# One semaphore per group for a GRU step's events, and PSUM zeroing moved behind tanh

## What is computed

```python
def step(hprev, gxt):
    gh = hprev @ whh.T + bhh
    r = jax.nn.sigmoid(gxt[:, :h] + gh[:, :h])
    z = jax.nn.sigmoid(gxt[:, h:2 * h] + gh[:, h:2 * h])
    n = jnp.tanh(gxt[:, 2 * h:] + r * gh[:, 2 * h:])
    hn = (1.0 - z) * n + z * hprev
    return (hn, hn)
...
fwd = _bigru(x_inner, ...)
bwd = jnp.flip(_bigru(jnp.flip(x_inner, 1), ...), 1)
y = jax.nn.silu(fwd + bwd) * jax.nn.silu(z)
```

## Time and profile before

| | |
|---|---|
| median of three executions | 1217.28 us |
| the profiled execution | 1218.96 us |
| its span, first to last instruction | 1217.2 us |
| mean granted TensorE clock | 0.582 of full speed |
| busy: PE, PE weight loads, DVE, ACT, POOL | 1088.6, 860.1, 948.2, 773.7, 154.8 us |
| recurrence of L2, first to last h_hi scan | 293.5 to 721.9 us |
| recurrence of L3, first to last h_hi scan | 765.2 to 1193.2 us |

### The profile page before, as it was taken

The page is one execution under the profiler, slowest core; times in us unless marked ns, Lnnn a source line. Parts: engine busy times, 40 slices in busy tenths (PEclk is TensorE's granted clock), DMA queues, the critical chain, the costliest instruction groups (busy, mean ns, idle before and its releaser), DMA issues. The chain is left out here.

```text
span 1217.2 us, 57599 instructions
## 1 busy us (share of the span) xinstructions
PE 1088.6 (89%) x22424; PEld 860.1 (71%) x22424; DVE 948.2 (78%) x5703; ACT 773.7 (64%) x4503; POOL 154.8 (13%) x222
## 2 busy tenths in 40 slices
PE   3787799949999999999999989999999999999997
PEld 2554354445888888888887866788888888888876
DVE  3543699987888888888888876788888888888884
ACT  4224530007777777777777764777777777777773
POOL 1001379920000000010001000000000001000100
PEclk9587899957555555555555556555555555555555
DMA  4000500000000000000000000000000000000000
GB/s 120 2 1 12 131 1 1 1 2 6 4 4 3 4 4 4 4 3 4 4 3 4 4 3 6 4 4 4 3 4 4 4 3 4 4 4 4 4 4 27
DMA packets 8235, 12.72 MB, mean 10 GB/s; under 512 B 5745, under 2 KB 7121, under 8 KB 7674
## 3 DMA queue, kind: packets, MB, share of 16 engines
q1 hardware_dynamic: 7962, 9.05, 3.0%
HBM read 8.26 MB, written 0.79 MB: 7 GB/s over the span
## 5 line engine op out<-in xcount | busy, mean ns | idle before, releaser
L1074 DVE TENSOR_TENSOR_SCAN L2s_h_hi<-L2s_renew,L2s_terms 96x32 f16<-96x32 f32 x512 | 113.2, 221 | 71.1 <-ACT L2s_terms L1134 9.3
L1074 DVE TENSOR_TENSOR_SCAN L3s_h_hi<-L3s_renew,L3s_terms 96x32 f16<-96x32 f32 x512 | 113.2, 221 | 70.9 <-ACT L3s_terms L1134 9.3
L1182 PE MATMUL L3s_reset_sum<-L3s_h_hi,L_w_hidden 97*128 97x8 f16 x2048 | 141.0, 179 | 20.9 <-DVE L3s_h_hi L1074 8.9
L1182 PE MATMUL L2s_reset_sum<-L2s_h_hi,L_w_hidden 97*128 97x8 f16 x2048 | 141.0, 179 | 20.5 <-DVE L2s_h_hi L1074 8.4
L1182 PEld LDWEIGHTS L3s_reset_sum<-L3s_h_hi,L_w_hidden 97*128 97x128 f16 x2048 | 94.5, 107 | 78.7 <-DVE L3s_h_hi L1074 32.0
L1182 PEld LDWEIGHTS L2s_reset_sum<-L2s_h_hi,L_w_hidden 97*128 97x128 f16 x2048 | 94.5, 107 | 78.5 <-DVE L2s_h_hi L1074 31.2
L1109 POOL TENSOR_TENSOR L_y<-L_states 96x64 f32<-96x64 f32 x128 | 40.8, 353 | 857.1 <-DVE L_states L1076 857.1
L1125 ACT ACTIVATE L3s_reset<-L3s_reset_sum 96x16 f32<-96x16 f32 x512 | 92.4, 181 | 67.0 <-PE L3s_reset_sum L1182 7.6
L1125 ACT ACTIVATE L2s_reset<-L2s_reset_sum 96x16 f32<-96x16 f32 x512 | 92.4, 181 | 66.7 <-PE L2s_reset_sum L1182 6.8
L1134 ACT ACTIVATE L2s_terms<-L2s_cand 96x16 f32<-96x16 f32 x512 | 111.2, 217 | 30.9 <-DVE L2s_cand L1059 4.5
L1134 ACT ACTIVATE L3s_terms<-L3s_cand 96x16 f32<-96x16 f32 x512 | 111.3, 217 | 30.1 <-DVE L3s_cand L1059 3.4
(11 more groups left out here) (257 smaller groups left out, 3522.7 us busy)
## 6 DMA issues: line engine op xcount, KB each, us to landing
L_wih_raw<-in_L_wih SPq DMA_DIRECT2D x2, 1152.0 KB, 11.3
l_w_raw<-in_L_w SPq DMA_DIRECT2D x1, 1296.0 KB
L_w_hidden_raw<-in_L_whh SPq DMA_DIRECT2D x2, 576.0 KB
stream<-in_x SPq DMA_DIRECT2D x2, 384.0 KB, 3.9
out<-stream SPq DMA_DIRECT2D x4, 192.0 KB, 2.1
l_idft<-in_idft SPq DMA_DIRECT2D x1, 400.0 KB
rpe_lw<-in_rpe_lw SPq DMA_DIRECT2D x1, 384.0 KB
l_dft<-in_dft SPq DMA_DIRECT2D x1, 288.0 KB, 2.9
```

The source lines that it names most:

```text
L1074: e.tensor_tensor_scan(flat(h_hi[g][0:C, x]), flat(renew[g][:, x]), flat(terms[g][:, x]), 0.0, ALU.mult, ALU.add).then_inc(hi_ready[g], 1)
L1182: return e.matmul(dst, weights.hidden[0:rows, wp, GATES * (2 * g + j) + gate, :], rhs, start=False, stop=False, skip_group_check=True)
```

## The change

Four edits, all in gru_steps.

1. The semaphores activated and cand_summed, and the kept part's raise of updated, become one semaphore per group, advanced. It is raised five times a step: by TensorE when the candidate's sum is complete, by ACT behind the reset sigmoid, the keep sigmoid and tanh, and by DVE behind the kept part. The candidate waits for the second of them, the kept part for the third, new_state for the fifth, each with a single wait. The semaphore updated is raised once a step.
2. The two copies of zeros no longer stand between renew sigmoid and tanh of step 0. The copy for the reset bank stands behind tanh of step 0, that for the keep bank behind tanh of step 1.
3. TensorE waits for each copy on a new semaphore, zeroed. In step 1 of these chunks it takes the gates in the order CAND, KEEP, RESET and waits ahead of RESET; in step 2 it keeps the order RESET, CAND, KEEP and waits ahead of KEEP.
4. The input products ahead for KEEP are spread over steps 2 to 7 of a chunk instead of 1 to 7.

The candidate's result stays in SBUF, as before.

```diff
-        reset_summed, keep_summed, cand_summed = each("reset_summed"), each("keep_summed"), each("cand_summed")
-        activated, cand_ready = each("activated"), each("cand_ready")
+        reset_summed, keep_summed = each("reset_summed"), each("keep_summed")
+        advanced, cand_ready = each("advanced"), each("cand_ready")
         updated, hi_ready, lo_ready = each("updated"), each("hi_ready"), each("lo_ready")
+        zeroed = each("zeroed")
+        RESET_ZEROED, KEEP_ZEROED = 0, 1
...
-                    e.wait_ge(activated[g], 3 * q + 1)
-                    e.wait_ge(cand_summed[g], q + 1)
+                    e.wait_ge(advanced[g], 5 * q + 2)
...
-                    e.wait_ge(activated[g], 3 * q + 2)
+                    e.wait_ge(advanced[g], 5 * q + 3)
                     e.tensor_tensor(terms[g][:, x, :, 1], keep[g][:, x], states[g][:, q, :, 1], ALU.mult)\
-                        .then_inc(updated[g], 1)
+                        .then_inc(advanced[g], 1)
...
-                    e.wait_ge(activated[g], 3 * q + 3)
-                    e.wait_ge(updated[g], 2 * q + 1 + BEFORE[g])
+                    e.wait_ge(advanced[g], 5 * q + 5)
...
-                    e.wait_ge(updated[g], 2 * q + 2 + BEFORE[g])
+                    e.wait_ge(updated[g], q + 1 + BEFORE[g])
...
-                    renewed = s == 0 and 1 <= q // STEPS < CHUNK_COUNT - 1
+                    renewed = 1 <= q // STEPS < CHUNK_COUNT - 1
...
-                        if renewed:
-                            e.activation(reset_sum(g, 1 - p)[0:C], zeros[:], ACT.Copy)
-                            e.activation(keep_sum(g, 1 - p)[0:C], zeros[:], ACT.Copy)
-
                         e.wait_ge(cand_ready[g], q + 1)
-                        e.activation(terms[g][:, x, :, 0], cand[g][:, x, :, 1], ACT.Tanh).then_inc(activated[g], 1)
+                        e.activation(terms[g][:, x, :, 0], cand[g][:, x, :, 1], ACT.Tanh).then_inc(advanced[g], 1)
+                        if renewed and s == RESET_ZEROED:
+                            e.activation(reset_sum(g, 1 - p)[0:C], zeros[:], ACT.Copy).then_inc(zeroed[g], 1)
+                        if renewed and s == KEEP_ZEROED:
+                            e.activation(keep_sum(g, 1 - p)[0:C], zeros[:], ACT.Copy).then_inc(zeroed[g], 1)
...
-                        for gate in (RESET, CAND, KEEP):
+                        before, at = divmod(q - 1, STEPS)
+                        zeroing = 1 <= before < CHUNK_COUNT - 1 and at in (RESET_ZEROED, KEEP_ZEROED)
+                        for gate in (CAND, KEEP, RESET) if zeroing and at == RESET_ZEROED else (RESET, CAND, KEEP):
+                            if zeroing and gate == (RESET if at == RESET_ZEROED else KEEP):
+                                e.wait_ge(zeroed[g], 2 * (before - 1) + (1 if at == RESET_ZEROED else 2))
                             for j in range(2):
                                 add(gate, 0, 0, j)
                                 add(gate, 1, 0, j)
-                        ahead(RESET, 1)
+                        ahead(RESET, RESET_ZEROED + 1)
...
-                        add(CAND, 0, 1, 1).then_inc(cand_summed[g], 1)
-                        ahead(KEEP, 1)
+                        add(CAND, 0, 1, 1).then_inc(advanced[g], 1)
+                        ahead(KEEP, KEEP_ZEROED + 1)
```

More of the change, by code:

```diff
@@ L1046, in _ @@
                 e.wait_ge(prepared, PREPARED)
-                for s, n in ((updated[1], 2), (hi_ready[0], 1), (hi_ready[1], 1), (lo_ready[0], 1)):
+                for s, n in ((updated[1], 1), (hi_ready[0], 1), (hi_ready[1], 1), (lo_ready[0], 1)):
                     e.sem_inc(s, n)
-                BEFORE = (0, 2)
+                BEFORE = (0, 1)
                 def candidate(g, q):
@@ L1093, in _ @@
                     new_state(1, q)
-                e.wait_ge(updated[1], 2 * SEQ + BEFORE[1])
+                e.wait_ge(updated[1], SEQ + BEFORE[1])
             @block.gpsimd
@@ L1102, in _ @@
                     for g in range(GROUPS):
-                        e.wait_ge(updated[g], 2 * (q + STEPS) + (0, 2)[g])
+                        e.wait_ge(updated[g], q + STEPS + (0, 1)[g])
                     for t in (q, SEQ - q - STEPS):
@@ L1120, in _ @@
                     x = q % 2
-                    renewed = s == 0 and 1 <= q // STEPS < CHUNK_COUNT - 1
+                    renewed = 1 <= q // STEPS < CHUNK_COUNT - 1
                     for g in range(GROUPS):
                         e.wait_ge(reset_summed[g], q + 1)
-                        e.activation(reset[g][:, x, :, 1], reset_sum(g, p)[0:C, :, s], ACT.Sigmoid).then_inc(activated[g], 1)
+                        e.activation(reset[g][:, x, :, 1], reset_sum(g, p)[0:C, :, s], ACT.Sigmoid).then_inc(advanced[g], 1)
                         e.wait_ge(keep_summed[g], q + 1)
-                        e.activation(keep[g][:, x], keep_sum(g, p)[0:C, :, s], ACT.Sigmoid).then_inc(activated[g], 1)
+                        e.activation(keep[g][:, x], keep_sum(g, p)[0:C, :, s], ACT.Sigmoid).then_inc(advanced[g], 1)
                         e.activation(renew[g][:, x, :, 1], keep_sum(g, p)[0:C, :, s], ACT.Sigmoid, scale=-1.0)
-                        if renewed:
-                            e.activation(reset_sum(g, 1 - p)[0:C], zeros[:], ACT.Copy)
-                            e.activation(keep_sum(g, 1 - p)[0:C], zeros[:], ACT.Copy)
                         e.wait_ge(cand_ready[g], q + 1)
-                        e.activation(terms[g][:, x, :, 0], cand[g][:, x, :, 1], ACT.Tanh).then_inc(activated[g], 1)
+                        e.activation(terms[g][:, x, :, 0], cand[g][:, x, :, 1], ACT.Tanh).then_inc(advanced[g], 1)
[3 more added lines that the diff above has]
+                            e.activation(keep_sum(g, 1 - p)[0:C], zeros[:], ACT.Copy).then_inc(zeroed[g], 1)
             @block.tensor
```

## The result

The changed kernel takes 1206.23 us (median of four executions, 1204.24 to 1208.04), the kernel before beside it 1218.47 us (four, 1216.33 to 1220.68). The ratio is 0.9891, with a 95% interval from 0.9871 to 0.9911. The forecast was 1203.3 us with a range from 1200.5 to 1211. Profile against profile the difference is 1218.96 - 1204.91 = 14.05 us, where the sum of the terms was 14.0.

A forecast was written before the change was run, and what follows sets the result against it. The recurrences' 0.81 us half-step loop, with no engine full, was taken to bound the kernel, plus disturbances. Gains of 5.8 + 8.6 = 14.4 us, kept as 14.0, gave 1203.3 us against the median 1217.28; range 1200.5 to 1211.

The forecast's parts named there:

- Zeroing, 5.8 us: Copies of zeros ahead of tanh at step 0, chunks 1 to 16: moving them returns 0.18 us each, 5.8 us.
- the late instructions: DVE instructions in the recurrences starting late although inputs are there: 28 a layer, 0.15 us each on average.
- Cost 0 for the reset sigmoid: On ACT, the other group's reset sigmoid behind tanh and one copy: not delayed, cost 0, at worst 4.8 us.
- TensorE's wait, 0: Two waits per group and chunk on TensorE for the copies: already met when asked, cost 0, at most 3.6 us.
- POOL's chunks, 0: Chunks 17 to 30, where POOL's additions cover the zeroing: moving the copies gains 0 (2.82 against 2.81 us).
- One semaphore, 8.6 us: DVE's candidate and new_state get one wait each: 2048 separate waits go, the sequencer runs ahead, 8.6 us gained.
- rival B: Each 128th DVE instruction is hitched whatever it is; only the count falls: 5.8 + 2.4, 1209.1 us, chance 0.17.
- rival C: Late DVE instructions have nothing to do with the count; the zeroing's 5.8 us alone: 1211.5 us, chance 0.12.
- Rival E: One counter raised by three engines hands on later, at the cand scan behind the reset sigmoid: 1234 us, chance 0.03.
- the disturbances: Recurrence time beyond undisturbed 0.813 us half-steps, from zeroing, POOL and late DVE instructions: 13.0 and 12.6 us by layer.
- the 0.4 us by which 14.4 was cut to 14.0: Cut from the summed gain because some late instructions fall into POOL's stretch, which has its own limit.

The follow-up runs named there:

- two-operation kernel: The changed kernel with two further DVE operations a half-step, each writing zeros into one column, both behind the kept part: 1203.99 us in one execution.

## Why the prediction was right

- **Zeroing, 5.8 us.** The price of one was right: 0.18 forecast, 0.19 measured with the late instructions out of the way. Its worth depends on the order: 4.2 us alone, 6.6 us when taken off last. The forecast didn't see that the late instructions and the copies cover part of each other. This did no harm to the sum.
- **Cost 0 for the reset sigmoid.** Right, with less room than assumed. Tanh's issue is 0.12 us, between the bounds 0.10 and 0.17, so 0.03 us are left and not 0.05. Both copies behind one tanh show what a held reset sigmoid costs: 5.9 us a layer.
- **TensorE's wait, 0.** Right: 0.10 us from the keep to the reset products, with the wait between them.
- **POOL's chunks, 0.** Right on the zeroing, 2.82 us before and after. The 0.37 us a chunk were POOL's own; without the additions 0.35 came back.
- **One semaphore, 8.6 us.** It measured 7.4 us alone and 9.7 last. The first half of the working was a count, and its period of 128 instructions of DVE is confirmed: every late one stands at the same place in 128, and with six instructions a half-step the pattern came back after four chunks and not eight. Of the 28 a layer 24 are late, since one kind of seven isn't. The second half was the guess that waits are the cause, since ACT shows no such thing. Two operations in place of the two waits settle it: same count, same number of instruction packets, no lateness, 421.3 us, and packets that come 1.7 us earlier. That rules out rival B (gain by the count, 1209.1 us); the fixed place in 128 rules out rival C (no tie to the count, 1211.5 us). The working was drawn too sharply in one point: even raises that wait for nothing bring back 1.6 to 1.9 us a layer.
- **Rival E.** No counter hands on later: an undisturbed half-step is 0.813 us before and after.
- **The size.** Profile against profile 14.05 us came out of 14.0. That is less of a proof than it looks. The 8.6 us were no count but what was left of the disturbances when zeroing and POOL were taken off, so the sum had to come out once both went, however they share it. And the 0.4 us by which 14.4 was cut to 14.0 had a wrong reason: late instructions cost as much in POOL's stretch as outside it (chunk 22 of L2 took 13.71 us before and 13.39 after, chunk 6, where 0.18 were the zeroing's, 13.51 and 13.01). The closeness there is luck. The medians differ by 12.2, and 1206.23 lies inside the range, 2.9 above the forecast; the recurrences, where all edits lie, give 13.9, and the rest is the scatter of whole executions, whose part ahead of L2 alone moved by up to 5.6 us between kernels that are alike there.

What stays open is what holds the sequencer at each 128th instruction. The packets show that a block of instructions is fetched around there. That fetching is the cause is inferred from the place and from the smaller lead. It wasn't tried whether two operations where the waits stood would be as harmless as behind the kept part. Nor was it tried whether one separate wait costs less at another place of the half-step, for instance right ahead of the kept part, which has slack.

## What to carry to other kernels

An operation that waits on two semaphores can cost more than a hand-over, even when one of its two events always comes before the other. Here one wait became an instruction of its own that held the engine's sequencer until it was met, and at each 128th instruction what came next was late. Where an engine's loop sets the time, let the producers of one operation's inputs raise one counter, if the order of the events in it is fixed, so that each operation has one wait. A short operation moved off a chain must be fitted into a gap that has been measured: the gap behind tanh held one copy of 0.20 us and not two, and the gap ahead of h_hi held additions that cost 0.37 us a chunk when another engine did them.

## What the runs showed of the hardware that was not expected

**Separate waits and the instruction stream.** The price of a late instruction depends on which other instructions are in the stream: DVE is idle before a late h_hi for 0.46 us with separate waits and for 0.21 us with separate raises; with operations in their place none is late. Per layer that is 4.6 to 5.1, 1.6 to 1.9 and 0 us. The Trainium skill, page "Runtime: NRT & Kernel Launch", section "Instruction fetch mechanics", says that fetching is hidden because the sequencer dispatches more slowly than blocks arrive. The two-operation kernel agrees with that, with 98 packets of instructions and no lateness; the kernels with separate waits are late with the same number of packets, which start 0.67 us behind the late instruction and not 1.0 us ahead of it. So if fetching is the cause, the rule holds only where the sequencer runs ahead.

**POOL beside DVE.** Four additions on POOL, 1.28 us long, lengthened DVE's kept product from 0.17 to 0.34 us, h_hi from 0.22 to 0.32, the states scan from 0.20 to 0.39 and one h_lo from 0.15 to 0.22, and cost 0.37 us on the path, though POOL itself has nothing that DVE waits for. Without them all of DVE's durations were ordinary (h_hi at most 0.222 us). The Trainium skill, page "SBUF — State Buffer", section "Who interferes with whom", says that a DVE instruction with two inputs in SBUF contends with a GpSimd instruction that reads SBUF, one with at most one such input doesn't (outside DVE's two-port modes), and that the shared port pair is an exclusive lock. The rows agree: the lengthened four read both inputs from SBUF, the candidate scan with one input in PSUM took 0.19 us beside them. They were held by 0.08 to 0.19 us, less than the 0.32 us (1.28 / 4) of one POOL addition, so each met only a part of one.
